# A sparse-expert sandwich block on one core: gathers and scatters of GpSimd gated in proportion to TensorE's steps, the second part's one-hots made one token tile a step

## The reference

```python
x = x + layernorm(attention_block(layernorm(x)))
x = x + layernorm(expert_block(layernorm(x)))

def expert_block(x):                       # E = 16 experts, TOP_K = 4, F = 512
    logits = -dist2(x, keys) + x @ rw.T + rb
    topv, topi = top_k(logits, 4)
    w = softmax(topv)
    hidden = gelu(einsum('bld,efd->blef', x, w1) + b1)
    exp_out = einsum('blef,edf->bled', hidden, w2) + b2
    return sum over the 4 chosen experts of w * exp_out
```

## Time and profile before

| | us |
|---|---|
| median of 3 runs (lowest, highest) | 698.85 (696.63, 700.03) |
| span of the profiled execution, first to last instruction | 694.4 |
| its own time outside the span | not recorded; the median lies 4.45 above its span |
| expert steps, first matmul of step 0 to first of step 157 | 237.87 to 659.85 |
| TensorE busy, of the span | 536.4 (77%) |
| VectorE, ScalarE, GpSimd busy | 364.9, 353.7, 281.1 |
| gathers L592: 128, sum and mean | 125.5, 0.98 |
| scatters L600: 128, sum and mean | 128.3, 1.00 |

### The profile page before, as it was taken

One profiled execution on the slowest core, in us unless ns is written; L12 is line 12 of the kernel. 1 busy time (PEld: TensorE's weight loads), 2 busy tenths in 40 slices (PEclk: granted clock), 3 DMA queues, 4 the chain that ended last, 5 costly groups with the idle time before them and its releaser, 6 DMA issues.

```text
span 694.4 us, 19926 instructions
## 1 busy us (share of the span) xinstructions
PE 536.4 (77%) x6242; PEld 481.6 (69%) x6242; DVE 364.9 (53%) x1325; ACT 353.7 (51%) x1079; POOL 281.1 (40%) x308
## 2 busy tenths in 40 slices
PE   4999879994502789977678789789977776679984
PEld 4967779993401489976677679678967776668942
DVE  6554779997999356545434553112334432233126
ACT  6524167775556365546445667336634434335513
POOL 4000000000451543566666743664566666645520
PEclk9999999998655799999999999999999989989998
DMA  8970000006001455444444645445866644546553
GB/s 229 255 280 9 3 3 0 0 0 243 1 1 76 120 161 157 138 131 131 131 140 143 204 124 162 135 144 146 264 207 180 183 130 133 145 122 192 174 197 122
DMA packets 55746, 92.28 MB, mean 133 GB/s; under 512 B 10352, under 2 KB 26096, under 8 KB 55152
## 3 DMA queue, kind: packets, MB, share of 16 engines
q1 hardware_dynamic: 45424, 72.35, 35.0%
q0 software_dynamic: 10240, 18.89, 9.2%
HBM read 78.07 MB, written 17.37 MB: 137 GB/s over the span
## 4 chain that ended last, share of the span: by engine, by line
PE 43%; issue 18%; DVE 18%; POOL 8%; ACT 7%; DMA 2%; DVEq 2%; another core or an unknown queue 0%; POOLq 0%; SPq 0%; ACTq 0%
PE bank L2148 15%; PE bank L2141 13%; POOL yd L600 6%; ACT value L883 3%; DVE shared L1187 2%; DVE shared L1179 2%; POOL shared L592 2%; DVE early L1467 2%; PE bank L1735 2%; DMA shared<-yd 1%; PE bank L1772 1%; PE bank L1840 1%; PE bank L1762 1%; PE bank L2133 1%; PE bank L2089 1%
## 5 line engine op out<-in xcount | busy, mean ns | idle before, releaser
L883 ACT ACTIVATE value<-bank,shared 128x128 f32<-128x128 f32 x632 | 180.8, 376 | 203.0 <-PE bank L2141 156.7
L2148 PE MATMUL bank<-shared,value 128*128 x1264 | 182.7, 290 | 62.4 <-ACT value L883 41.7
L2148 PEld LDWEIGHTS bank<-shared,value 128*128 128x128 f32 x1264 | 161.7, 200 | 76.7 <-issue 76.1
L2141 PE MATMUL bank<-early,shared 128*128 x1264 | 180.9, 288 | 5.3 <-issue 2.8
L592 POOL DMA_INDIRECT shared<-xd,early x128 | 125.5, 980 | 127.5 <-PE bank L2141 79.8
L2141 PEld LDWEIGHTS bank<-early,shared 128*128 128x128 f32 x1264 | 162.6, 200 | 9.3 <-issue 8.4
L1663 DVE SCALAR_TENSOR_TENSOR early<-bank,value,early 128x128 f32 x158 | 55.4, 351 | 195.8 <-PE bank L2148 116.6
L600 POOL DMA_INDIRECT yd<-early x128 | 128.3, 1002 | 67.8 <-DVE early L1663 36.2
L560 POOL TENSOR_TENSOR shared<-shared,xn 128x512 f32<-128x512 f32 x4 | 5.1, 1264 | 174.9 <-DVE xn L1262 167.1
L2133 PE MATMUL bank<-ident,shared 128*128 128x128 f32 x128 | 35.9, 284 | 9.0 <-DMA shared<-xd,early 5.7
L2003 PE MATMUL bank<-ksp,shared 128*128 128x32 bf16 x1536 | 40.9, 177 | 0.0
(11 more groups left out here) (334 smaller groups left out, 689.3 us busy)
## 6 DMA issues: line engine op xcount, KB each, us to landing
shared<-w1b SPq DMA_DIRECT2D x158, 258.0 KB
w1b<-in_w_t SPq DMA_DIRECT2D x1, 4096.0 KB, 17.8
shared<-col_dram SPq DMA_DIRECT2D x1, 4096.0 KB, 13.4
shared<-in_w_t SPq DMA_DIRECT2D x1, 4096.0 KB, 12.3
att<-yd SPq DMA_DIRECT2D x8, 512.0 KB
shared<-yd SPq DMA_DIRECT2D x4, 1024.0 KB, 9.1
xd<-xnT SPq DMA_DIRECT2D x2, 1280.0 KB
shared<-xd,early POOLq DMA_INDIRECT x128
```

The lines of the kernel that those rows point to most:

```text
L883: ins = act.activation(hT[:, i % 2, tok(c)], bank[2 + i % 2][:, tok(c)], ACT.Gelu, bias=w1_now[:, i % WR, F + c:F + c + 1])
L2141: ins = mm(bank[2 + i % 2][:, tok(c)], w1_now[:, i % WR, tok(c)], x_now, start=True, stop=True)
L2148: ins = mm(bank[6 + i % 2][:, 0:D], hT[:, i % 2, tok(c)], w2_sb[:, bass.ds(e, 1), c, :] .rearrange("p a d -> p (a d)"), start=(c == 0), st ...
```

## The change

The constant `NEAR` goes and `HEAD = 4` comes; `BEHIND` is 34. Every DMA of GpSimd's queue, gather or scatter, now waits by its place in the queue: number k (from 0 to 255) waits until (k - 4) * 158 // 256 first products are done. A scatter keeps its waits for results too. The one-hots take one token tile a step, steps 44 to 59, with `lane_hots` ahead of `tile_hots`, and `row_list(1)` is made in step 62. `LIST_STEP`, and with it the steps in which TensorE transposes tiles 64 to 68, stays.

```diff
     RING = 8
     SLOTS = 32
     LEAD = 3
-    BEHIND = 27
+    BEHIND = 34
     GRP = 4
     XR = 24
-    NEAR = 8
+    HEAD = 4
...
         def hots_of(i):
             j = i - HOT_STEP
-            return TS + j // 3 * 2 + j % 3 if 0 <= j < 3 * TS // 2 and j % 3 < 2 else None
+            return TS + j if 0 <= j < TS else None
...
+            moved = [0]
+
+            def in_step():
+                freed(pool, up_ps, (moved[0] - HEAD) * IALL // (2 * JALL))
+                moved[0] += 1
+
             def rows(n):
-                if n >= NEAR:
-                    pool.wait_ge(up_ps, step_of(n) - NEAR + 1)
+                in_step()
...
             def results(m):
+                in_step()
                 pool.wait_ge(y_ready, step_of(m) + E)
...
-                elif i == LIST_STEP:
+                elif i == HOT_STEP + TS + 2:
                     row_list(1)
                 if hots_of(i):
+                    lane_hots(hots_of(i))
                     tile_hots(hots_of(i), 1)
-                    lane_hots(hots_of(i))
```

## The result

The changed kernel takes **673.17 us** (median of 4 runs, 668.43 to 676.96) against 699.44 for the kernel before: a ratio of 0.963, 95% interval 0.958 to 0.968. The forecast was 679.5 in a range of 666 to 701. The profiled execution took 668.43 us, its span is 666.4.

A forecast was written before the change was run, and what follows sets the result against it. POOL's back-to-back DMA issues, holding TensorE's signals, were taken to bound the kernel; -23.3 for pace and +4 for one-hots gave -19.3, a span of 675.1, and with 4.45 carried along 679.5 us, range 666 to 701.

The forecast's parts named there:

- What bounds the kernel: Expert steps: while POOL issues DMAs back to back, TensorE's signals are held and arrive together once POOL has paused.
- The pace: Expert steps: DMAs spread at 1.62 a step give 2.57 us a step for 146 steps, -23.3 us.
- VectorE's one-hots: Steps 44 to 59: five more one-hot blocks make the second product wait for y_add, +4 us, between 0 and 6.0.
- The gather for tile 64: Step 72: opened at step 68, its wait goes; the gain is part of that stretch's -5.9 us.
- Scatters 34 behind: POOL's queue: each first scatter is opened when its sum is ready, no work moved; costed at nothing.
- The added wait: POOL's queue: the up_ps wait each scatter gains stands before a wait it already has; costs 0.
- first steps: Start: a shorter first burst and tile 8 a step later, both within 2 us with opposite signs; 0.
- One: Expert steps: the pause is TensorE's, two steps take 5.3 us, 2.73 a step, 703 or about 699 us; chance 0.13.
- Two: Expert steps: three DMAs in a row hold signals as long as four; slower, 728 us; chance 0.07.
- Three: Gathers or yg slots late: three to four misses of 3.1 us give +11, 690 us; chance 0.12.
- Four: Steps 44 to 59: busy VectorE stretches POOL's DMA issues, 20 us, 699 us; chance 0.02.
- Five: Expert steps: bursts of three break up, nothing is held, 2.3 us a step, about 640 us; chance 0.04.

The follow-up runs named there:

- NEAR 12: The kernel before with every gather opened four steps earlier: 725.45 us, ratio 1.037 on the first chip; 731.2 us, ratio 1.040 on the third.
- HEAD 8: The changed kernel with every DMA opened four places earlier: 613.11 us, ratio 0.949 on the second chip; 700.47 us, ratio 1.001 on the third.
- The scatters by SyncE: The changed kernel with POOL's indirect scatters replaced by plain SP copies in sorted order (output rows wrong): 611.03 us, ratio 0.946 on the second chip.
- the packed placement of one-hots: The changed kernel with one-hots two steps in three from 44, then every step to 64, list at 66: 611.36 us, ratio 0.948 on the second chip.

## Why the prediction was right, step by step

**What bounds the kernel.** That POOL's bursts hold TensorE's signals was read from one cycle of before. The runs bear it out on chips that hold: shorter bursts with the same 256 DMAs gain 3 to 4%, longer ones lose (NEAR 12: +4% twice), and a burst of seven leaves ACT idle for 7.9 us. As a rule it was put too strictly: a signal given in a burst's first DMA came through in 57 of 61 cases (both traces together), and 22 of 127 later ones did. And the granted clock has no term in it, though TensorE's busy time fell by 11.1 us.

**The pace, -23.3 us.** I forecast 2.57 us a step. Steps 4 to 149 took 616.99 - 246.07 = 370.92 us; without the 16 steps with one-hots, (370.92 - 43.02) / 130 = 2.52. The cycle was built as n x 1.28 + 1.0 for two steps, and as a time for a cycle it stood: four DMAs 6.13 (6.12 by that), three 4.76 (4.84). What was simplified is that every cycle has two steps. Sixteen bursts of two, 3.10 us for 1.56 steps, run at 1.99 a step. This is the mis-sized term: 0.05 x 146 = 7 us too slow. The last seven steps took 14.4 us for 13.7. Stretch by stretch the forecast of -22.2 for the longest met -23.1, and +6.6 met +5.4.

**VectorE's one-hots, +4 us.** Steps 44 to 59 took 43.02 us, 2.69 a step: 2.7 us over sixteen at 2.52. Against the change without this part it was 2.5. Inside the bounds of 0 to 6, one third below what I took. VectorE in those steps was busy 29.27 us; forecast were 30.2. The path was another than forecast. The second product waited for `y_add` just once there, 0.6 us; TensorE's `table` (L2079 in the changed file) waited for the one-hot rows themselves, 1.8 us in two waits, of which one is

```profile
PE bank L2079 <- DVE xnT L1473: 1.1, 1, 1.1
```

and TensorE's busy time there was 0.9 us longer, with 20 more small matmuls for five more token tiles (37.16 for 36.30). In the kernel without this part no wait of `table` stands in these steps. So the size came out near, but not by the path that was reasoned; that part is luck.

**The gather for tile 64.** It was issued at 410.66, had landed by 413.06 and was first used at 421.89. The step that took 5.03 us is gone, and steps 72 to 85 gave the forecast 5.9 us to a tenth. What I had not said is that the earlier list also lets POOL's queue move on in steps 60 to 71 and so makes them slower; the run without the one-hot part shows that the two cancel. The whole third part of the change is worth nothing measurable.

**Scatters 34 behind, at nothing.** As a cost it was nothing. That 27 would let a scatter stand before gathers was foreseen, but not its size: 712.05 against 669.96 us, 6%, is what separates 27 from 34 under the gate. I had expected a small gain from the gate alone.

**The added wait, first steps.** Both at nothing, and next to nothing was found: the pause between DMAs stays 0.30 with `up_ps` among the waits; the time before step 4 fell by 1.6 us.

**The sum.** -19.3 forecast, -28.0 measured. Of the 8.7 between, 7 are the pace, 1.3 VectorE, 1.1 the ends, less 0.7 in the last steps. The median lies 6.8 above the profiled span, where I carried 4.45 along.

**Rivals.** *One* (a cycle is always two steps of TensorE's, 5.3 us) fell: cycles of three took 4.7. Its sum has a slip: 0.76 x 5.3 + 0.24 x 6.1 is 5.49, or 2.75 a step and not 2.73, which makes it about 705 us. *Two* (threes hold as long as fours) fell with it, though its break-even of 2.69 us a step was just 0.17 away. *Three* (late gathers or slots): the wait for rows is 1.0 us. It fell on early tiles: TensorE took tile 7's rows 3.12 us after the gather's issue and had waited 0.66 us for them. The Trainium skill's fit (DMA: Bandwidth & Descriptors, Anatomy of one DMA) gives an estimate of 2.2 us for a gather; tile 64's took 2.41 from issue to landing, a little more, and tile 7's more still, since at 2.46 us TensorE began to wait for it. *Four* (VectorE keeps POOL from issuing): with VectorE busy 29.27 of 43.02 us, 27 DMA issues took 27.11 us, 1.00 each as before. So what the Trainium skill says of a lock (SBUF - State Buffer, Who interferes with whom) does not show here either; it speaks of VectorE's two-port modes, and no row tells whether VectorE was in one. *Five* (nothing held, 640 us) did not come on this chip, but on the second chip the change's relatives run with nothing held, though their bursts do not break up.

**What stays open.** What makes the second chip different: one chip behaved that way and two others, and the runs of the result, the other way; whether it is the chip itself or a state that it was in was not tried. The kernel before left no trace there; that its 646 us come from pair stretches bound by POOL's 2 x 1.28 = 2.56 us a step is an estimate (94 x 2.56 + 59 x 2.0 = 359 us against 153 x 1.62 x 1.28 = 317, 41 for 33 measured between it and HEAD 8). If it is so, spreading the DMAs pays on either chip, for two different reasons. Whether it is POOL's issuing that holds the signals, or the transfers that follow it, no run separates: on a chip that holds, the two never came apart. The scatters by SyncE were not run on a chip that holds, where they would tell most; nor was the packed placement of one-hots. No version was shown to beat the change.

## What to carry to other kernels

Where one engine's DMA issues come in runs, count them per step of the bounding engine and compare the pace of stretches with one, with two and with a mixture: the cost was not linear in the number, and spreading 256 DMAs evenly gave 3 to 4% with no work removed. A gate by the consumer's progress helps only if every other wait in the same queue is already met when its turn comes; here the gate alone was 2% slower, and the longer distance alone 2.6% (on the chip that holds nothing). And when a mechanism rests on when signals arrive, run the kernel before beside each experiment on the same chip and look at its trace: one edit was 5% faster than before on one chip and no faster on another. Before a row of a wait table is compared across two kernels, match the instructions by the program's order: here part of the waits for gelu stood under "issue".

## What the runs showed of the hardware

- On the chips that held, most signals that TensorE gave while POOL issued indirect DMAs back to back reached ScalarE only about 1 us after the last of them had ended (median 1.03 us in the trace before, 0.94 in the changed kernel's). Gelu then started 1.34 us after its product with a burst of three, 2.75 with four, 7.3 with seven, in the cycles shown. Signals given in a burst's first DMA mostly came through (18 of 18 and 39 of 43), and of later ones 8 of 52 and 14 of 75; with bursts of six (NEAR 12), 28 of 63.
- VectorE was kept waiting too: where TensorE's second product ended later than a burst's first DMA and VectorE stood ready, `y_add` began a median of 2.7 us after it in 18 cases of the changed kernel in which it ran after the burst, for 0.6 us as a rule outside of bursts and 0.95 at most within them on the second chip (HEAD 8). ScalarE's signal to TensorE was not held: in the few cases of each trace in which TensorE waited for a gelu that ended in such a place, the second product started 0.15 to 0.5 us after it, as elsewhere.
- On another chip of the same type the same instructions with the same issue times (0.97 to 0.99 us and 0.30 between) held nothing in a burst of 137; its kernel before took 646 us against 699 to 701.
- An indirect DMA of 128 rows costs POOL 0.98 to 1.00 us of issue in the mean (single ones 0.94 to 1.73) and 0.30 to the next, with one, two or three waits and on each chip alike.
- The granted clock of TensorE was 0.95 over the expert steps before and 1.00 in the changed kernel; 2696 and 2695 matmuls took 340.0 and 328.9 us of busy time.
